# Expert choice stage: fp16 halves with three products, or single fp32 numbers with fp32 products

## The chip, the cores and the metric

The kernel runs on one core of a Trainium2 chip. A core has five engines with queues of their own that meet only at semaphores: TensorE (PE; its weight loads have a row of their own, PEld), VectorE (DVE), ScalarE (ACT), GpSimd (POOL) and SyncE (SP), which here issues nearly all DMAs. Matmul results land in PSUM, everything else is in SBUF. The metric is the device time of one execution in microseconds, as a median over runs.

## The reference

A residual stream `x` of 128 sequences x 64 tokens x 128 features goes through four steps: a gated cross attention (8 heads), a gated expert choice feed-forward, a second cross attention (16 heads) and a routed feed-forward (2 of 8 experts). The change concerns the second step:

```python
b, n, d = x.shape                                   # 128, 64, 128, after a layer norm
gate_logits = jnp.einsum('bnd,ed->ben', x, gate_query)
affinity = _sinkhorn(gate_logits / jnp.exp(log_temp))        # 16 experts
gates, idx = jax.lax.top_k(affinity, CAP)                    # CAP = 32 tokens of each sequence
expert_in = jnp.take_along_axis(x[:, None, :, :], idx[..., None], axis=2)
h = jax.nn.gelu(jnp.einsum('becd,edf->becf', expert_in, w1) + b1[None, :, None, :])   # 128 -> 512
expert_out = jnp.einsum('becf,efd->becd', h, w2) + b2[None, :, None, :]               # 512 -> 128
out = jnp.zeros_like(x).at[jnp.arange(b)[:, None, None], idx].add(gates[..., None] * expert_out)
```

## The kernel before

The program has five stages in a row: attention `a0` (with the expert weights loaded beside it), the Sinkhorn iterations and the top-k (`expert_choice`), `run_experts`, attention `a1`, and the routed layer. `run_experts` is where nearly all of the change lies.

**Numbers in two halves.** An fp32 value is kept as two fp16 numbers, `hi` (the value rounded) and `lo` (the value less `hi`). `matmul3` (L236 to L241) makes a product of three fp16 matmuls, hi·hi, hi·lo and lo·hi. The expert weights are split once, in `a0`: SP loads each expert's `w1` and `w2` into a buffer `rawe`, and POOL writes `hi` by a copy (L809) and `lo` by a subtraction (L812), one such step in each of 64 units; SP waits for POOL (`ew_lo`) before it loads over `rawe`.

**The steps of run_experts.** The 128 sequences make 8 groups of 16. A step is one expert `e` of one group `G`, 128 steps in all, and each covers 16 x 32 = 512 gathered rows. The order on each engine is written out by hand in `body(a)`; a step's work on PE is

- in every second step `take` (L1601): four fp16 matmuls with a one-hot matrix gather the rows of the next tile of tokens into the accumulators `psR` and `psH[:, 3]`;
- the first layer of the next step's expert (L1640): for each `ft` of 4, 128 of the 512 hidden features of 512 rows into the bank `psH[:, ft]`;
- the second layer of this step's expert (L1650): 4 row blocks `r` x 4 `ft` products of 128x128 into the one bank `psE`;
- in every second step the scatter of the last two experts (L1674): one-hot matrices `put` times the gated rows `eo` are added up in `psA`, in pairs for the two halves of 64 partitions.

ACT makes `g32` by the gelu of each `psH` bank (L1722) and rounds two of them at a time to `h` hi (L1727); it also makes the hi halves of the gated rows (L1706) and of the gathered rows (L1710). DVE makes the lo halves: of `h` (L1803, twice a step), of the gated rows (L1821) and of the gathered rows (L1773). DVE further makes `put` (L1816), `sel` (L1761) and the gating (L1830), which copies `psE` out times the gates. PE waits for `h_lo` and for `gated` of the step before ahead of the second layer, for `eo_lo` and `put` ahead of the scatter. `h`, `put` and `eo` have two buffers, `psE` and `eo32` have one.

Ahead of the steps, for the 8 tiles of the first group (L1611 to L1620, `take_early`), PE gathers rows into the four `psH` banks, two for hi and two for lo, ACT copies three of them out and DVE one.

## Time and profile before

| | us |
|---|---|
| median of 3 runs | 1879.14 (1878.74 to 1879.46) |
| the profiled execution | 1880.83 |
| its span, first to last instruction | 1878.1 |
| first matmul of `run_experts`' steps to the last of its scatter | 476.8 to 1256.8 |

| engine | busy over the span | share |
|---|---|---|
| PE | 1796.1 | 96% |
| DVE | 1613.5 | 86% |
| ACT | 1548.2 | 82% |
| POOL | 662.4 | 35% |

The mean granted clock of TensorE is 0.978 of full. PE's busy time counts a matmul from its start to the end of its way through the array, so two that overlap are counted once, and the distance of starts in a stream (called the pitch below) is much shorter than the duration of one: what a stream costs is its count times its pitch. POOL is idle in the whole of `run_experts`.

### The profile page before, as it was taken

To read this page: it belongs to the slowest core of one execution; us is meant where nothing else is said; L and a number is where in the kernel's file an instruction comes from. 1 tells how busy PE (TensorE), PEld (TensorE's weight loads), DVE (VectorE), ACT (ScalarE), POOL (GpSimd) and SP (SyncE) were. 2 spreads that over 40 slices of the span, in tenths; PEclk is the share of its full clock that TensorE was granted. 3 is DMA by queue.
4 is the path that set the end of the run, shared out by engine and by line. 5 is a ranking of instruction groups with operands and counts; after the bars stand their busy time and mean duration, and the time that the engine had idled before them with its cause. 6 is when DMAs were issued, how large, how long until landed. Compare 5 with 4: busy or idle time off the path is not lost. (4 is left out here: it accounts for less than half of the span.)

```text
span 1878.1 us, 72670 instructions
## 1 busy us (share of the span) xinstructions
PE 1796.1 (96%) x28635; PEld 1312.8 (70%) x28635; DVE 1613.5 (86%) x3645; ACT 1548.2 (82%) x2773; POOL 662.4 (35%) x918
## 2 busy tenths in 40 slices
PE   6999998896999999999999999989999999999898
PEld 4777776642577777777776777766777777777587
DVE  5999998598788888889898988778999999988754
ACT  5999997475999999999999999868888888888443
POOL 3788887332000000000000000006666666655565
PEclk9999999897999999999999999999999999999799
DMA  6645444487000000000000002005665555533233
GB/s 174 141 95 101 96 94 88 152 307 270 15 13 15 13 15 13 13 13 12 16 10 18 10 15 50 2 15 128 165 158 154 147 152 152 146 71 69 64 116 120
DMA packets 312953, 160.66 MB, mean 86 GB/s; under 512 B 236558, under 2 KB 295862, under 8 KB 312374
## 3 DMA queue, kind: packets, MB, share of 16 engines
q1 hardware_dynamic: 312278, 157.95, 32.1%
q8 instruction: 129, 2.11, 0.5%
q14 instruction: 66, 0.54, 0.1%
q10 hardware_dynamic: 480, 0.05, 0.0%
HBM read 62.33 MB, written 36.83 MB: 53 GB/s over the span
## 5 line engine op out<-in xcount | busy, mean ns | idle before, releaser
L240 PEld LDWEIGHTS psE<-ew,h 128*128 128x128 f16 x6144 | 353.3, 98 | 33.4 <-DVE h L1803 4.6
L240 PE MATMUL psE<-ew,h 128*128 128x128 f16 x6144 | 364.0, 219 | 2.2 <-DVE h L1803 2.1
L1803 DVE TENSOR_TENSOR h<-g,h 128x1024 f16<-128x1024 f32 x256 | 312.8, 1222 | 49.8 <-ACT h L1727 47.9
L1722 ACT ACTIVATE g<-psH,eb1T 128x512 f32<-128x512 f32 x512 | 325.0, 679 | 10.3 <-PE psH L240 4.3
L815 POOL TENSOR_TENSOR Ph<-E,Ph 128x512 f16<-128x512 f32 x192 | 222.0, 1156 | 233.6 <-ACT Ph L769 233.6
L1876 POOL MEMSET rbias<- 64x384 f32 x1 | 0.4, 411 | 801.8 <-POOLq L133 801.8
L1727 ACT ACTIVATE h<-g 128x1024 f16<-128x1024 f32 x256 | 270.6, 1057 | 8.2
L721 ACT ACTIVATE vB<-psV 128x512 f16<-128x512 f32 x384 | 225.9, 589 | 51.0 <-PE psV L619 48.8
L842 DVE TENSOR_TENSOR vB<-psV,vB 128x512 f16<-128x512 f32 x384 | 248.2, 677 | 1.1 <-ACT vB L721 1.0
L619 PE MATMUL psV<-shared 96*64 96x512 f16 x1536 | 210.9, 381 | 1.4 <-DVE vB L842 1.3
L821 POOL TENSOR_TENSOR E<-E,rden 128x512 f32<-128x512 f32 x192 | 199.7, 1040 | 15.5 <-DVE rden L853 14.8
L240 PE MATMUL psH<-shared,ew 128*128 128x512 f16 x768 | 178.9, 382 | 0.4 <-DVE xg L1773 0.2
L240 PE MATMUL psH<-xg,ew 128*128 128x512 f16 x768 | 177.5, 379 | 0.4
L674 PE MATMUL psY<-vB,PT 128*64 128x128 f16 x4608 | 164.2, 221 | 4.9 <-DMA PT<-Ph 4.3
L861 DVE TENSOR_REDUCE top<-psS 128x8 f32<-128x512 f32 x192 | 131.7, 686 | 37.3 <-PE psS L698 36.7
L674 PEld LDWEIGHTS psY<-vB,PT 128*64 128x64 f16 x4608 | 144.9, 111 | 19.6 <-DMA PT<-Ph 10.6
L759 ACT ACTIVATE E<-E,zero_col 128x512 f32<-128x512 f32 x192 | 137.9, 718 | 18.6 <-DVE E L864 15.0
L864 DVE TENSOR_TENSOR E<-psS,top 128x512 f32<-128x512 f32 x192 | 132.7, 691 | 7.8
L698 PE MATMUL psS<-shared,xTa 128*64 128x256 f32 x1024 | 134.6, 383 | 2.0 <-DVE E L864 1.9
L240 PEld LDWEIGHTS psH<-shared,ew 128*128 128x128 f16 x768 | 71.3, 98 | 92.2 <-issue 17.5
L851 DVE TENSOR_REDUCE den<-E 128x8 f32<-128x512 f32 x192 | 130.0, 677 | 4.4 <-ACT E L759 3.5
L240 PEld LDWEIGHTS psH<-xg,ew 128*128 128x128 f16 x768 | 70.8, 98 | 88.3 <-issue 11.6
(312 smaller groups left out, 3385.6 us busy)
## 6 DMA issues: line engine op xcount, KB each, us to landing
keys_ahead<-shared SPq DMA_DIRECT2D x52, 512.0 KB, 4.9
shared<-keys_ahead SPq DMA_DIRECT2D x52, 512.0 KB, 3.6
rawe<-in_L_ffn_w_dram SPq DMA_DIRECT2D x32, 256.0 KB, 3.1
wb<-rw SPq DMA_DIRECT2D x64, 128.0 KB, 2.0
idx<-places SPq DMA_DIRECT2D x110, 64.0 KB, 2.6
out_dram<-x SPq DMA_DIRECT2D x7, 512.0 KB, 3.2
context_T<-shared SPq DMA_DIRECT2D x64, 48.0 KB, 2.4
PT<-Ph SPq DMA_TRANSPOSE x192, 2.9
```

The source lines that it names most:

```text
L240: last = e.matmul(to, a, b, start=start and n == 0, stop=stop and n == 2, **flags)
L619: last = e.matmul(a.values(b)[half(hp)], cT[:, a.ring, cl, half(b)], Bw[:, bl, a.g, hp].rearrange("p k d -> p (k d)"), start=n == 0, stop= ...
L674: last = e.matmul(psY[half(b), 0:D], PT[:, a4.par, pl, pair, half(b)], vB[:, a4.par, vl, b, pair, :], start=a4.g == n == pair == 0, stop=a ...
L698: last = e.matmul(psS[half(b), h:h + 4, :], xT[:, a.tp, half(b)], u[:, a.slot, h:h + 4, half(b)], start=True, stop=True)
L721: e.activation(vB[:, a.par, 0, b].rearrange("p k d -> p (k d)"), a.values(b), ACT.Copy).then_inc(s["vh" + name], 1)
L759: e.activation(E[:, a1.four], E[:, a1.four], ACT.Exp, bias=zero_col[:], scale=DH ** -0.5)\
L815: e.tensor_tensor(Ph[:, a2.par, 1].rearrange("p k t -> p (k t)"), E[:, a2.four].rearrange("p h l -> p (h l)"), Ph[:, a2.par, 0].rearrange( ...
L821: e.tensor_tensor(E[:, a1.four], E[:, a1.four], rden[:, a1.par, :].unsqueeze(2).broadcast_to([P, 8, N]), ALU.mult)\
L842: e.tensor_tensor(vB[:, a.par, 1, b].rearrange("p k d -> p (k d)"), a.values(b), vB[:, a.par, 0, b].rearrange("p k d -> p (k d)"), ALU.sub ...
L1722: e.activation(g32[:, ft, :], psH[:, ft, :], ACT.Gelu_apprx_tanh, bias=b1T[:, a.expert(1) * FT + ft:a.expert(1) * FT + ft + 1]).then_inc(s ...
L1727: e.activation(h[:, 1 - par, 0, ft - 1:ft + 1, :], g32[:, ft - 1:ft + 1, :], ACT.Copy).then_inc(s["h_hi"], 1)
L1803: e.tensor_tensor(h[:, 1 - par, 1, 2 * q:2 * q + 2, :], g32[:, 2 * q:2 * q + 2, :], h[:, 1 - par, 0, 2 * q:2 * q + 2, :], ALU.subtract)\
```

## The change

In `run_experts` each value is one fp32 number. The expert weights are loaded by SP straight into their place, and the POOL steps that split them are gone, as are SP's waits for them. `matmul3` of both layers gives way to one fp32 matmul of the same shape. The gelu writes `h` in fp32 itself; the rounding of `h` and both subtractions are gone. The gating writes `eo` in fp32 straight into one of two buffers, with no halves after it; `put` is fp32 too. The gathered rows, still gathered by fp16 matmuls of two halves that add up in one accumulator, are copied out as fp32 by DVE alone (by ACT and DVE in turn ahead of the steps, where `take_early` now adds both halves up in one pair of banks).

```diff
-            self.w1 = sb(c, "ew1", [P, 2, NE, DFF], F16)
-            self.w2 = sb(c, "ew2", [P, 2, NE, FT, D], F16)
+            self.w1 = sb(c, "ew1", [P, NE, DFF], F32)
+            self.w2 = sb(c, "ew2", [P, NE, FT, D], F32)
...
-                        if first and a.on:
-                            turn = a.j.mod(4)
...
-                            if turn % 2 == 0:
-                                wait(e, s["ew1" if turn == 0 else "ew2"], n, 16)
-                                e.tensor_copy(hi, rawe[:, turn // 2]).then_inc(s["ew_hi"], 1)
-                            else:
-                                wait(e, s["ew_hi"], n, 2, turn // 2 - 1)
-                                e.tensor_tensor(lo, rawe[:, turn // 2], hi, ALU.subtract).then_inc(s["ew_lo"], 1)
...
-                                last = matmul3(e, psH[:, ft, :],
-                                               [w1[:, hl, a.expert(1), ft * P:ft * P + P] for hl in range(2)],
-                                               [a.rows(hl, 1) for hl in range(2)])
-                                last.then_inc(s["H"], 1)
+                                e.matmul(psH[:, ft, :], w1[:, a.expert(1), ft * P:ft * P + P], a.rows(1),
+                                         start=True, stop=True).then_inc(s["H"], 1)
...
-                            wait(e, s["h_lo"], j, 2)
+                            wait(e, s["gelu"], j, FT)
...
-                                    last = matmul3(e, psE[:, r, :],
-                                                   [h[:, par, hl, ft, r * P:r * P + P] for hl in range(2)],
-                                                   [w2[:, hl, a.expert(0), ft, :] for hl in range(2)],
-                                                   r == ft == 0, ft == FT - 1, skip_group_check=True)
+                                    last = e.matmul(psE[:, r, :], h[:, par, ft, r * P:r * P + P],
+                                                    w2[:, a.expert(0), ft, :], start=r == ft == 0,
+                                                    stop=ft == FT - 1, skip_group_check=True)
...
-                                    for hl in range(2):
-                                        for bp in range(2):
-                                            rows = slice(64 * bp, 64 * bp + 64)
-                                            last = e.matmul(psA[:, bp, r, :], put[rows, buf, r, :], eo[rows, buf, hl, r, :],
+                                    for bp in range(2):
+                                        rows = slice(64 * bp, 64 * bp + 64)
+                                        last = e.matmul(psA[:, bp, r, :], put[rows, buf, r, :], eo[rows, buf, r, :],
...
-                                e.activation(g32[:, ft, :], psH[:, ft, :], ACT.Gelu_apprx_tanh,
+                                e.activation(h[:, 1 - par, ft, :], psH[:, ft, :], ACT.Gelu_apprx_tanh,
...
-                            low_rows(a)
+                            wait(e, s["g"], a.t, 2)
+                            side, bank = (1, psH[:, 3, :]) if a.bp == 0 else (0, psR[:])
+                            e.tensor_copy(rows_of(a, side), bank.rearrange("p (e c) -> p e c", c=CAP))\
+                             .then_inc(s["g_1"], 1)
...
-                            wait(e, s["eo_lo"], j - 1)
+                            wait(e, seeded["A"], j - 2)
...
-                            e.tensor_tensor(eo32[:], psE[:], g4.unsqueeze(2).broadcast_to([P, RT, D]),
+                            e.tensor_tensor(eo[:, par], psE[:], g4.unsqueeze(2).broadcast_to([P, RT, D]),
```

PE's order in two steps in the midst of the first group, first before and then after. `shared` holds the gathered rows of the even groups, `ew_1` the expert weights; the number behind the x is that of matmuls in a row.

```order
L1674 MATMUL psA<-eo,put 128x128 x32
L1606 MATMUL psR<-sel,xne 128x512
L1606 MATMUL psH<-sel,xne 128x512
...
L240 MATMUL psH<-shared,ew_1 128x512 x12
L240 MATMUL psE<-ew_1,h 128x128 x48
```

```order
L1655 MATMUL psA<-eo,put 128x128 x16
L1593 MATMUL psR<-sel,xne 128x512
L1593 MATMUL psH<-sel,xne 128x512
...
L1625 MATMUL psH<-shared,ew_1 128x512 x4
L1633 MATMUL psE<-ew_1,h 128x128 x16
```

Nothing changes its place on PE: a third of the matmuls of both layers stands there, and half of those of the scatter.

DVE's order over one step with a tile to gather, before and then after, with `h` the hidden values, `xg` the gathered rows and `eo` the gated rows.

```order
L1773 TENSOR_TENSOR xg<-psH,xg 128x16x32
L1747 TENSOR_SCALAR xnfe<-x,mean,rstd 128x128
L1816 TENSOR_SCALAR put<-iota,tok_slot 128x128 x4
L1821 TENSOR_TENSOR eo<-eo_1,eo 128x512
L1803 TENSOR_TENSOR h<-g_1,h 128x1024
L1761 TENSOR_SCALAR sel<-idx_1,token_of_p 128x512
L1830 TENSOR_TENSOR eo_1<-psE,gate_slot 128x512
```

```order
L1760 COPY xg<-psH 128x16x32
L1712 TENSOR_SCALAR xnfe<-x,mean,rstd 128x128
L1769 TENSOR_SCALAR put<-iota,tok_slot 128x128 x4
L1726 TENSOR_SCALAR sel<-idx_1,token_of_p 128x512
L1778 TENSOR_TENSOR eo<-psE,gate_slot 128x512
```

The three subtractions of DVE are gone or have become the one copy, and the rest has kept its order.

## Rows read from the trace of the kernel before

**Rows 1.** Stretches: length, busy PE, PEld, DVE, ACT, POOL; then clock, DMA share, GB/s.
```profile
476.80:484.90 8.10, 7.07 (x26) 2.65 (x24) 3.71 (x6) 6.74 (x11) 0.00 (x0) 0.79 0.08 26
484.90:1253.90 769.00, 767.05 (x9955) 554.25 (x9956) 673.87 (x1378) 709.25 (x1052) 0.00 (x0) 1.00 0.05 15
```

**Rows 2.** All waits of PE from 500 to 1200: total us, times, longest.
```profile
PE psE L240 <- DVE h L1803: 0.2, 1, 0.2
```

**Rows 3.** Timeline of PE, two steps: start, us, work [idle].
```profile
700.86 2.75 PE L240 MATMUL psH<-shared,ew 128*128 128x512 f16 x12
703.45 2.84 PE L240 MATMUL psE<-ew,h 128*128 128x128 f16 x48
706.23 1.07 PE L1674 MATMUL psA<-eo,put 64*128 64x128 f16 x32
707.13 0.38 PE L1606 MATMUL psR<-sel,xne 64*128 64x512 f16 x1
...
707.66 2.76 PE L240 MATMUL psH<-shared,ew 128*128 128x512 f16 x12
710.26 2.84 PE L240 MATMUL psE<-ew,h 128*128 128x128 f16 x48
712.94 0.81 PE L240 MATMUL psH<-shared,ew 128*128 128x512 f16 x3
```

**Rows 4.** Groups of PE, whole span: weights, moving operand, count, busy us, mean ns.
```profile
L240 PE MATMUL psE<-ew,h 128*128 128x128 f16 x6144 | 364.0, 219 | 2.2 <-DVE h L1803 2.1
L240 PE MATMUL psH<-shared,ew 128*128 128x512 f16 x768 | 178.9, 382 | 0.4 <-DVE xg L1773 0.2
L698 PE MATMUL psS<-shared,xTa 128*64 128x256 f32 x1024 | 134.6, 383 | 2.0 <-DVE E L864 1.9
```

**Rows 5.** Timeline of PE, three streams of fp32 matmuls in other stages.
```profile
411.61 1.12 PE L1426 MATMUL psZ<-raws,wTs 64*96 64x128 f32 x16
...
1803.30 1.04 PE L2174 MATMUL psHr<-wb,xTr 128*64 128x128 f32 x16
...
1805.54 0.60 PE L2156 MATMUL psTr<-ident,gr 128*128 128x128 f32 x4
```

**Rows 6.** Weight loads of three lines: ns min/median/max, first and last start.
```profile
L240 PEld LDWEIGHTS psE<-ew,h x6144: 95/98/99, 484.9 to 1253.9; 128*128 128x128 f16 x199
...
L2174 PEld LDWEIGHTS psHr<-wb,xTr x512: 132/137/231, 1766.0 to 1869.4; 128*64 128x64 f32 x171
...
L1426 PEld LDWEIGHTS psZ<-raws,wTs x32: 156/160/160, 411.6 to 431.8; 64*96 64x96 f32 x32
```

**Rows 7.** Groups of DVE and ACT: count, busy us, mean ns, idle before.
```profile
L1803 DVE TENSOR_TENSOR h<-g,h 128x1024 f16<-128x1024 f32 x256 | 312.8, 1222 | 49.8 <-ACT h L1727 47.9
L1727 ACT ACTIVATE h<-g 128x1024 f16<-128x1024 f32 x256 | 270.6, 1057 | 8.2
L1722 ACT ACTIVATE g<-psH,eb1T 128x512 f32<-128x512 f32 x512 | 325.0, 679 | 10.3 <-PE psH L240 4.3
L1830 DVE TENSOR_TENSOR eo<-psE,gate_slot 128x512 f32<-128x512 f32 x128 | 88.3, 690 | 41.3 <-PE psE L240 41.2
L1821 DVE TENSOR_TENSOR eo<-eo,eo 128x512 f16<-128x512 f32 x128 | 87.4, 683 | 0.0
```

**Rows 8.** Timeline of the intake and of both ends of the steps, [idle before].
```profile
471.00 1.58 ACT L1690 ACTIVATE shared<-psH 128x512 f16<-128x512 f32 x3 [0.22 <-PE psH L1597]
...
484.91 0.29 PE L240 MATMUL psE<-ew,h 128*128 128x128 f16 x2 [1.04 <-DVE h L1803]
...
1251.32 2.85 PE L240 MATMUL psE<-ew,h 128*128 128x128 f16 x48 [0.92 <-DVE h L1803]
...
1256.43 0.62 PE L1674 MATMUL psA<-eo,put 64*128 64x128 f16 x16 [1.71 <-DVE eo L1821]
```

**Rows 9.** Attention a0: a POOL group, and a PEld group from 40 to 310.
```profile
L812 POOL TENSOR_TENSOR ew<-rawe,ew 128x512 f32 x26 | 30.2, 1160 | 0.0
...
L619 PEld LDWEIGHTS psV<-Bw,shared 96*64 96x64 f16 x696 | 36.1, 110 | 27.5 <-DVE vB L842 8.8
```

More of the change, by code:

```diff
@@ L535, in body @@
                                 n = a.j.div(4)
-                                wait(e, s["ew_lo"], n, 2, -2)
                                 load_w2(e, n)
@@ L1523, in group, with rows, gathered @@
                     return self.G + (self.e + off) // NE
-                def rows(self, hl, off):
-                    return xg[self.group(off) % 2][:, hl, self.expert(off), :]
-            def gathered(parity, hl, batch):
-                return xg[parity][:, hl, :, CAP * batch:CAP * batch + CAP]
+                def rows(self, off):
+                    return xg[self.group(off) % 2][:, self.expert(off), :]
+            def gathered(parity, batch):
+                return xg[parity][:, :, CAP * batch:CAP * batch + CAP]
             def rows_of(at, side):
                 parity = (at.G + 1 + at.k // GT) % 2
-                return [gathered(parity, hl, (at.k % GT) * 2 + side) for hl in range(2)]
+                return gathered(parity, (at.k % GT) * 2 + side)
             def all_steps(eng, body):
@@ L1591, in batch_rows, with take_early @@
                         e.matmul(psR[:], pick[:, par, :], idx16[:], start=True, stop=True).then_inc(s["R"], 1)
-                    def take_early(k, hl):
-                        for side in range(2):
-                            q = slice(64 * side, 64 * side + 64)
-                            last = e.matmul(psH[:, 2 * hl + side, :], first_tiles[q, k, hl, :], sel[q, k % 2, :],
-                                            start=True, stop=True)
-                        last.then_inc(s["g"], 1)
+                    def take_early(k):
+                        for hl in range(2):
+                            for side in range(2):
+                                q = slice(64 * side, 64 * side + 64)
+                                last = e.matmul(psH[:, 2 * (k % 2) + side, :], first_tiles[q, k, hl, :], sel[q, k % 2, :],
+                                                start=hl == 0, stop=hl == 1)
+                        last.then_inc(s["g"], 2)
                     def take(par):
@@ L1668, in body @@
                                 wait(e, s["put"], j - n, RT)
[L1669 removed]
+                                wait(e, s["gated"], j - n)
                                 for r in range(RT):
[L1671 to L1676 removed]
+                                    for bp in range(2):
+                                        rows = slice(64 * bp, 64 * bp + 64)
+                                        last = e.matmul(psA[:, bp, r, :], put[rows, buf, r, :], eo[rows, buf, r, :],
+                                                        start=False, stop=a.e == NE and n == 1,
+                                                        skip_group_check=True)
                                 last.then_inc(s["A"], 1)
@@ L1686, in high, with first_rows @@
                         e.activation(xn[:, k % 2, 0], xnf[:, k % 2], ACT.Copy).then_inc(s["x_hi"], 1)
-                    def first_rows(k, hl, side):
-                        wait(e, s["g"], Step(None, 0, k), 2, hl - 1)
-                        return e.activation(gathered(0, hl, 2 * k + side),
-                                            psH[:, 2 * hl + side, :].rearrange("p (e c) -> p e c", c=CAP), ACT.Copy)
+                    def first_rows(k):
+                        wait(e, s["g"], Step(None, 0, k), 2)
+                        e.activation(gathered(0, 2 * k + 1), psH[:, 2 * (k % 2) + 1, :].rearrange("p (e c) -> p e c", c=CAP),
+                                     ACT.Copy).then_inc(s["g_1"], 2)
                     for k in range(GT):
@@ L1695, in _ @@
                             high(GT)
-                        first_rows(k, 0, 0)
-                        first_rows(k, 0, 1).then_inc(s["g_1"], 1)
-                        first_rows(k, 1, 1).then_inc(s["g_1"], 1)
+                        first_rows(k)
                     def body(a):
                         j, par = a.j, a.par
-                        if a.has(-1):
-                            wait(e, s["gated"], j - 1)
-                            wait(e, seeded["A"], j - 3)
-                            e.activation(eo[:, 1 - par, 0], eo32[:], ACT.Copy).then_inc(s["eo_hi"], 1)
-                        if a.has_tile(0):
-                            wait(e, s["g"], a.t, 2)
-                            side, bank = (1, psH[:, 3, :]) if a.bp == 0 else (0, psR[:])
-                            e.activation(rows_of(a, side)[0], bank.rearrange("p (e c) -> p e c", c=CAP), ACT.Copy)\
-                             .then_inc(s["g_1"], 1)
                         for ft in range(FT):
@@ L1765, in first_rows @@
                         wait(e, s["g"], Step(None, 0, k), 2)
-                        e.tensor_copy(gathered(0, 1, 2 * k), psH[:, 2, :].rearrange("p (e c) -> p e c", c=CAP))\
-                         .then_inc(s["g_0"], 2)
-                    def low_rows(a):
-                        side, bank = (1, psH[:, 3, :]) if a.bp == 0 else (0, psR[:])
-                        high, low = rows_of(a, side)
-                        wait(e, s["g_1"], a.t, 2, a.bp - 1)
-                        e.tensor_tensor(low, bank.rearrange("p (e c) -> p e c", c=CAP), high, ALU.subtract)\
+                        e.tensor_copy(gathered(0, 2 * k), psH[:, 2 * (k % 2), :].rearrange("p (e c) -> p e c", c=CAP))\
                          .then_inc(s["g_0"], 1)
```

70 lines of the change are left out of this document (21 added, 49 removed).

## The prediction

> **What bounds the kernel now.** I read the busy times by stretch first. In the 769 us of the expert steps PE is busy for 767.05 us at full clock, ACT for 709.25 and DVE for 673.87 [rows 1]. Three engines are near full, so busy time alone does not say which sets the pace; the waits do. From 500 to 1200 PE waits once, for 0.2 us [rows 2], while DVE sat idle for 47.9 us until ACT's `h` came [rows 7]. So PE's stream sets the time, and the timeline shows it unbroken: two steps take 712.94 − 700.86 = 12.08 us [rows 3]. ACT and DVE are close behind, but what they give up is worth only what PE waits for them. The question is then what an fp32 product costs PE against three fp16 ones.
>
> **What the fp16 products cost.** From the starts in [rows 3]: the first layer takes 2.59 us for 12 matmuls of 512 columns, a pitch of 216 ns. The second layer takes 2.68 us for 48 matmuls of 128 columns (710.26 to 712.94), 56 ns each. The scatter takes 0.90 us for 16 pairs, 56 ns a pair. The gather with what follows it takes 0.53 us and does not change. Check: 2 × 2.59 + 2 × 2.68 + 0.90 + 0.53 = 11.97; the other 0.1 is one late weight load between second layer and scatter, where 706.23 − 703.45 is 2.78, not 2.68. Another of 0.09 is inside the 0.53. Both stand where the array goes from full height to halves or back.
>
> **What an fp32 product costs.** Two things must be read, since no fp32 matmul of before has the new shapes.
> First, the number of records. The scores of the attention (L698) are four matmuls a unit in the source; for the 128 units of `a1` that is 512, and the trace has 1024 records of them [rows 4]. So an fp32 matmul is two passes.
> Second, the pitch of a pass. An fp32 pass of 256 columns lasts 383 ns, an fp16 one of 512 columns 382 [rows 4]: two cycles a column. The streams agree. 16 fp32 passes of 128 columns, in eight pairs beside each other, take 1.04 us; less 0.27 for the last one's duration that is 0.77 over seven pitches, 110 ns at L2174 [rows 5]; the L1426 stream, whose pairs split the rows as the scatter's do, gives (1.12 − 0.27) / 7 = 121 with the wait for its first load of 160 ns [rows 6] in it. 110 is twice the 56 ns. A whole fp32 matmul costs four cycles a column where three fp16 matmuls cost three.
> I take 109 ns for a pass of 128 columns. A pass of 512 columns is 1024 cycles, 427 ns at 2.4 GHz, and the fp16 pitch of 216 for 512 cycles has 2 to 3 ns on top: 429 ns.
>
> **The sum, for two steps.** First layer: 8 matmuls are 16 passes × 429 = 6.86 us, was 5.18: +1.68. Second layer: 32 matmuls are 64 passes × 109 = 6.98, was 5.36: +1.62. Scatter: 16 matmuls are 32 passes, 16 pairs × 109 = 1.74, was 0.90: +0.84. The two late loads become longer: fp32 loads last 137 and 160 ns for 64 and 96 columns [rows 6], 23 ns for 32 more, so about 185 for 128, an estimate, against 98: +0.09 each, +0.18. Together +4.32, so 16.4 us in place of 12.08. Over 64 pairs of steps: +276 us.
>
> **What is removed beside it.** The 256 roundings on ACT (270.6 us), the 256 subtractions of `h` (312.8) and the 128 of `eo` (87.4) go, with their like for the gathered rows [rows 7]. PE waited for them at three places at the ends only: 1.04 us before the first second layer, 0.92 and 1.71 near the last ones [rows 8]. The last of these is the gating's two halves, one of them a subtraction of 0.68 [rows 7], and I let about 1.3 of it go. Together −3.3 us. Everywhere else this cover is worth nothing, for PE did not wait.
> The new work of DVE is hidden. Before a step it needs the copy of the gathered rows (about 0.68 us, the time of a subtraction of the same size at L1821 [rows 7]), which PE awaits only ahead of `ft` 3, 2.6 us after the gather. The gating now waits for the scatter of two experts before, since `eo` has two buffers. That is new: behind it on DVE stand `split_tile` and the next copy. The wait ends half of a scatter (0.9 us) after the second layer; gating takes 0.69 more [rows 7], and PE next needs it 3.4 us of first layer later. No stall; if it did come, it would be under 1 us in each pair.
> The intake ahead of the steps goes by ACT's three copies, 1.58 + 0.22 us of idle for each of 8 tiles [rows 8]. One copy is left on ACT, but PE and DVE still hand each tile to and fro, with one copy, one comparison and one pick on DVE: I take −0.5 in all, with 0 and −5 as ends.
> In `a0` POOL loses 64 steps, the subtractions of 1160 ns among them [rows 9]. PE's loads wait 8.8 us there for DVE's `vB`, in part since the two share time; I take −2 and keep 0 and −6 as ends. The DMAs are as many and as large, and SP only loses waits.
>
> Sum: +276 − 3.3 − 0.5 − 2 = +270. Against the profiled execution's own 1880.83 (span 1878.1) that is 2151; the median of the runs is 1.7 lower: **2149 us**.
>
> **A rule and the row.** The streams above have weights of 64 or 96 columns; the second layer's have 128. The one fp32 stream with 128 columns, L2156, runs at (0.60 − 0.27) / 3 = 110 ns [rows 5], but those are transposes, so its loads may be of another kind. The Trainium skill (TensorE: Matmul & The Clock Gate, The mechanism) says that a weight load overlaps with a running matmul only when it goes to other rows of the array. By that rule a full-height load could not hide. For fp16 the trace speaks against it: loads of 98 ns run at a pitch of 56 [rows 3, 6]. The same page (Weight-path perf modes) says that fp32 weights don't get the fast load, and (LDWEIGHTS) that a load takes its columns over 1.2 GHz, by which 128 columns would be an estimate of 107 ns, just under the pitch that I use. The rule gives the first rival below.
>
> **The rivals.**
> *The load of 128 fp32 columns isn't hidden.* Then a pass of the second layer and of the scatter takes the load's length, 185 ns by the extrapolation above, not 109. For: load and pass are nearly equal, and no row has both at 128 columns. Against: 160 ns loads run at 110 in L1426, so a good part of their length isn't occupancy. Price: 4096 passes and 1024 pairs × 76 ns = +389, 2540 us. Chance 0.06.
> *An fp32 pass costs less than I read: one cycle a column.* This one ends faster. It is decided at the point where an fp32 product costs what three fp16 ones do, 648 ns for 512 columns and 168 for 128. Were the two cycles due to PSUM or the narrow weights of those stages and a pass of full weights ran at 216 and 56, PE would need 2 × (1.73 + 1.79) + 0.9 + 0.5 = 8.4 us for two steps, still above DVE's and ACT's new load (ACT eight gelus of 0.68, 5.4 us [rows 7]). Price: 64 × (8.5 − 12.08) = −229, 1650 us. Rows with wide and with narrow weights speak against it. Chance 0.02.
> *The three terms come out right, but TensorE's clock falls to the lower level for parts of the steps.* In rows it was low only where PE had been waiting (0.79 in the first 8 us [rows 1]), and PE now waits less. If a tenth of the steps were at half speed: +105, 2255. Chance 0.03.
> *PE isn't held by the products at all, and the time stays.* It needs slack in PE's stream that the rows don't show. 1879 ± 4. Chance 0.01.
>
> **How the numbers follow.** The forecast has 0.88. Its own range: a pitch of 111 instead of 109 adds 10 us, an occasional wait for the gating or the longer `put` 10 more; late loads that stay at 98 ns take 12 off, `a0` another 4, a shorter stay at the low clock 3. That is 2125 to 2172, which leaves out the rivals and a little of the forecast itself. A difference under 0.2% (4 us) can't be told from none here. Faster by more: 0.02. Within: 0.01. Slower: 0.97.
>
> **What would show it.** In the trace of after: PE without waits in the steps, DVE and ACT busy about half the time; records of the first layer 429 ns apart, of the second 109, pairs of the scatter 109; two steps in 16.4 us; a0 within a few us of before. It would be wrong if passes of the second layer stood 150 or more apart, if the granted clock fell, or if PE waited for gated rows.

## The result, and the profile of the kernel after

The kernel after takes **2161.27 us** (median of 4 runs, 2156.89 to 2164.07); the kernel before, run between them, took 1878.94 (4 runs). The ratio is 1.1501, with a 95% interval of 1.1481 to 1.1521. The forecast was 2149 with a range of 2125 to 2172: right in sign and nearly in size, 12 us too low. The profiled execution took 2161.61 us, its span 2159.3, against 1880.83 and 1878.1 before.

The first lines of the page of after, busy time and the span in 40 slices:

```profile
PE 2077.0 (96%) x26075; PEld 1542.3 (71%) x26075; DVE 1252.0 (58%) x3261; ACT 1185.1 (55%) x2261; POOL 609.0 (28%) x854
...
PE   6999998969999999999999999999899999999898
...
DVE  5999985972333332333333333221599999998754
ACT  5999984733333333333333333333488888888643
...
PEclk9999998989999999999999999999999999999899
```

In the long middle part, the expert steps, PE stays at 9 while ACT falls to 3 and DVE to 3 or 2. The same by stretches, to be held against [rows 1] (columns: the stretch and its length, then the busy time of PE, PEld, DVE, ACT and POOL with their instructions, the granted clock, the DMA share, GB/s). The first piece is the first 7 us of the steps:

```profile
472.40:479.40 7.00, 7.00 (x18) 3.15 (x17) 2.19 (x5) 4.89 (x8) 0.00 (x0) 1.00 0.14 40
479.40:1532.30 1052.90, 1052.84 (x7405) 779.08 (x7403) 320.47 (x995) 358.50 (x563) 0.00 (x0) 1.00 0.04 10
```

PE is busy for 1052.84 of 1052.90 us at full clock. DVE's 320.47 and ACT's 358.50 are 30% and 34% of that, where before they had 88% and 92%. The clock is at its upper level from the first step on; before it was 0.79 in the first 8 us [rows 1].

The waits from 490 to 1500 us (who waits, for whom: us in total, times, longest). Before, PE waited there once, for 0.2 us [rows 2]; now no row has PE in it, none of its weight loads (PEld) names another engine, and the three longest waits are for PE:

```profile
ACT h L1692 <- PE psH L1625: 668.1, 435, 6.5
DVE eo L1778 <- PE psA L1655: 359.4, 61, 6.9
DVE eo L1778 <- PE psE L1633: 297.8, 61, 6.5
```

Two steps on PE, the counterpart of [rows 3]: L1625 is the first layer, L1633 the second, L1655 the scatter, L1593 the gather (columns: start us, length us, what, number of records):

```profile
800.09 3.70 PE L1625 MATMUL psH<-shared,ew 128*128 128x512 f32 x8
803.63 3.73 PE L1633 MATMUL psE<-ew,h 128*128 128x128 f32 x32
807.20 3.60 PE L1625 MATMUL psH<-shared,ew 128*128 128x512 f32 x8
810.63 3.73 PE L1633 MATMUL psE<-ew,h 128*128 128x128 f32 x32
814.30 2.06 PE L1655 MATMUL psA<-eo,put 64*128 64x128 f32 x32
816.19 0.38 PE L1593 MATMUL psR<-sel,xne 64*128 64x512 f16 x1
...
816.72 0.70 PE L1625 MATMUL psH<-shared,ew 128*128 128x512 f32 x1
```

From 800.09 to 816.72 are 16.63 us, where it had been 12.08; 16.4 was forecast. A step's first layer is 4 matmuls in the source and has 8 records, its second 16 and has 32: two passes for each fp32 matmul, as read. From the starts, the two first layers take 3.54 and 3.43, the second 3.57 and 3.67, the scatter 1.89, the gather and what follows 0.53, the same as before.

The second layer's and the scatter's own groups (columns: line, engine, operation, shapes, count; busy us, mean ns of one; idle time before it). A load of 128 fp32 columns lasts 192 ns, a bit more than the 185 extrapolated from [rows 6]:

```profile
L1633 PE MATMUL psE<-ew,h 128*128 128x128 f32 x4096 | 478.0, 275 | 0.1
L1633 PEld LDWEIGHTS psE<-ew,h 128*128 128x128 f32 x4096 | 477.4, 192 | 61.0 <-issue 61.0
...
L1655 PE MATMUL psA<-eo,put 64*128 64x128 f32 x2048 | 131.4, 278 | 0.5 <-DVE put L1769 0.5
```

Taken over all starts in the trace, records of L1625 stand 429 ns apart, those of L1633 111.6, the pairs of L1655 111.9. The first is exactly the forecast. The other two are above the 109 taken from two cycles a column.

**Where the 281.2 us of span came from**, by the starts and ends of the stages in both traces:

| stretch | before | after | change | forecast |
|---|---|---|---|---|
| up to the intake (mostly a0) | 461.4 | 459.9 | −1.5 | −2 |
| intake | 15.4 | 12.6 | −2.8 | −0.5 |
| the steps | 780.0 | 1062.5 | +282.5 | +276 − 3.3 |
| all behind them | 621.2 | 624.2 | +3.0 | 0 |

The last line can't be put down to the change, which has no code there: in the other kernels below that stretch took from 618.8 to 623.0 us, so one trace of each kernel doesn't tell 3 us from scatter.

### The profile page after: what moved, and what is told of

It reads as the page before. It is cut to its first block and busy times, and to the rows that moved or that the text cites. A ratio compares the mean times of both kernels' runs of the same rounds, so it can differ in the third digit from the quotient of the medians.

```text
span 2159.3 us, 65740 instructions
## 1 busy us (share of the span) xinstructions
PE 2077.0 (96%) x26075; PEld 1542.3 (71%) x26075; DVE 1252.0 (58%) x3261; ACT 1185.1 (55%) x2261; POOL 609.0 (28%) x854
## 3 DMA queue, kind: packets, MB, share of 16 engines
q8 instruction: 109, 1.79, 0.3%
## 5 line engine op out<-in xcount | busy, mean ns | idle before, releaser
L1692 ACT ACTIVATE h<-psH,eb1T 128x512 f32<-128x512 f32 x512 | 351.9, 687 | 691.3 <-PE psH L1625 691.2
L1633 PEld LDWEIGHTS psE<-ew,h 128*128 128x128 f32 x4096 | 477.4, 192 | 61.0 <-issue 61.0
L1778 DVE TENSOR_TENSOR eo<-psE,gate_slot 128x512 f32<-128x512 f32 x128 | 88.5, 692 | 691.4 <-PE psA L1655 372.5
L1633 PE MATMUL psE<-ew,h 128*128 128x128 f32 x4096 | 478.0, 275 | 0.1
L1625 PE MATMUL psH<-xg,ew 128*128 128x512 f32 x512 | 233.6, 599 | 0.0
L1625 PE MATMUL psH<-shared,ew 128*128 128x512 f32 x512 | 233.4, 599 | 0.0
L1625 PEld LDWEIGHTS psH<-shared,ew 128*128 128x128 f32 x512 | 92.3, 190 | 105.9 <-issue 105.9
L1625 PEld LDWEIGHTS psH<-xg,ew 128*128 128x128 f32 x512 | 92.2, 190 | 103.0 <-issue 102.0
L757 ACT ACTIVATE E<-E,zero_col 128x512 f32<-128x512 f32 x192 | 137.8, 718 | 18.8 <-DVE E L851 15.4
L1655 PE MATMUL psA<-eo,put 64*128 64x128 f32 x2048 | 131.4, 278 | 0.5 <-DVE put L1769 0.5
```

The source lines that it names most:

```text
L757: e.activation(E[:, a1.four], E[:, a1.four], ACT.Exp, bias=zero_col[:], scale=DH ** -0.5)\
L1625: e.matmul(psH[:, ft, :], w1[:, a.expert(1), ft * P:ft * P + P], a.rows(1), start=True, stop=True).then_inc(s["H"], 1)
L1633: last = e.matmul(psE[:, r, :], h[:, par, ft, r * P:r * P + P], w2[:, a.expert(0), ft, :], start=r == ft == 0, stop=ft == FT - 1, skip_gro ...
L1692: e.activation(h[:, 1 - par, ft, :], psH[:, ft, :], ACT.Gelu_apprx_tanh, bias=b1T[:, a.expert(1) * FT + ft:a.expert(1) * FT + ft + 1]).the ...
```

## The experiments

Every kernel was compared with the kernel before on the same chip (1878.66 for the first four, 1879.71 for the next four, 1880.67 for the last). The theory was the forecast's: time is the number of PE's passes times their pitch, and the rest is off the path. Its first weak place was named in the prediction: whether a pass of 128 fp32 columns is spaced by its stream or by its load.

**Each part alone.** Three kernels start from before and take one part of the change each.

*The first layer alone*, with the gathered rows as single fp32 numbers copied by DVE:

```diff
-                                last = matmul3(e, psH[:, ft, :],
-                                               [w1[:, hl, a.expert(1), ft * P:ft * P + P] for hl in range(2)],
-                                               [a.rows(hl, 1) for hl in range(2)])
-                                last.then_inc(s["H"], 1)
+                                e.matmul(psH[:, ft, :], w1[:, a.expert(1), ft * P:ft * P + P], a.rows(1),
+                                         start=True, stop=True).then_inc(s["H"], 1)
```

> The kernel before with the first layer alone in fp32 (expert w1, gathered rows, intake), second layer and scatter in fp16 halves. If the time is PE's stream and the terms add up: the trace of after has 16 passes of 429 ns and one late load of 0.1 us more in two steps, 6.97 us against 5.18, so +1.79 x 64 = +115 us, less some 5 for the intake and the start: 1879 + 110 = 1989. By the prediction's own term it would be +107 - 3: 1983. Rival: the parts don't add up, since each alone leaves ACT and DVE nearly as busy as before and PE then waits for them: over 2000.

*The second layer alone*, where the gelu writes `h` as fp32:

```diff
-                                    last = matmul3(e, psE[:, r, :],
-                                                   [h[:, par, hl, ft, r * P:r * P + P] for hl in range(2)],
-                                                   [w2[:, hl, a.expert(0), ft, :] for hl in range(2)],
-                                                   r == ft == 0, ft == FT - 1, skip_group_check=True)
+                                    last = e.matmul(psE[:, r, :], h[:, par, ft, r * P:r * P + P],
+                                                    w2[:, a.expert(0), ft, :], start=r == ft == 0,
+                                                    stop=ft == FT - 1, skip_group_check=True)
```

> The kernel before with the second layer alone in fp32 (w2, h; no rounding of h, no subtraction). PE's stream: 64 passes of 111.6 ns, 7.14 us against 5.36 in two steps, +1.78 x 64 = +114, less 3 at the ends: 1990. By the prediction's pitch of 109 it would be +104 - 3: 1980. The pitch of the passes says which: 111 to 112 or 109. Rival: the relief of ACT (270 us) and DVE (313 us) gives something back and it comes out under 1975.

*The scatter alone*, with `eo` and `put` in fp32:

```diff
-                                    for hl in range(2):
-                                        for bp in range(2):
-                                            rows = slice(64 * bp, 64 * bp + 64)
-                                            last = e.matmul(psA[:, bp, r, :], put[rows, buf, r, :], eo[rows, buf, hl, r, :],
...
+                                    for bp in range(2):
+                                        rows = slice(64 * bp, 64 * bp + 64)
+                                        last = e.matmul(psA[:, bp, r, :], put[rows, buf, r, :], eo[rows, buf, r, :],
```

> The kernel before with the scatter alone in fp32 (put, eo; no halves of eo). PE's stream: 1.89 us against 0.90 in two steps, +0.98 x 64 = +63, less 2 at the end: 1940. By the prediction's term +0.84 + 0.09: +60 - 2 = 1937. The three single parts together should give the whole change, +282: rival, the whole is more or less than the sum of its parts by over 15 us.

Measured, each a median of four: 1987.93 (ratio 1.0582, 1.0564 to 1.0600), 1987.58 (1.0580, 1.0563 to 1.0598) and 1936.69 (1.0313, 1.0296 to 1.0331), so +109, +109 and +58 us. Together that is +276 of the +282 of the whole. The parts add up, as they must if one engine's stream is the only thing that counts; a part that had been hidden under another's wait would have shown as a gap here. Most of the 6 us between them has a source in the traces. The steps of the three kernels grow by 111.7, 108.2 and 58.7 us, where 64 times what two of their steps grow by would be 117.3, 114.0 and 63.0. So each sheds 4 to 6 us of small waits and low clock, 16 in sum, where the whole can shed its 9 only once. One step of the first and of the second on PE:

```profile
805.11 3.70 PE L1639 MATMUL psH<-xg,ew 128*128 128x512 f32 x8
808.65 2.84 PE L240 MATMUL psE<-ew,h 128*128 128x128 f16 x48
811.33 3.65 PE L1639 MATMUL psH<-xg,ew 128*128 128x512 f32 x8
```

```profile
805.60 2.76 PE L240 MATMUL psH<-xg,ew 128*128 128x512 f16 x12
808.20 3.73 PE L1650 MATMUL psE<-ew,h 128*128 128x128 f32 x32
811.77 2.75 PE L240 MATMUL psH<-xg,ew 128*128 128x512 f16 x12
```

In the first, the fp16 second layer keeps its 2.68 us (808.65 to 811.33); in the second, the fp16 first layer keeps its 2.60 (805.60 to 808.20) and the fp32 second layer has the 3.57 of after. A part's cost hardly depends on the format of its neighbour: two steps grow by 1.83, 1.78 and 0.98 us in the three, 4.60 in sum, and by 4.55 in the whole.

**What the helpers of ACT and DVE were worth.** This kernel starts from before and leaves out the subtractions that make the low half of `h`; PE multiplies the high half in their place, the same number of matmuls.

```diff
-                            wait(e, s["h_lo"], j, 2)
+                            wait(e, s["h_hi"], j, 2)
...
-                                                   [h[:, par, hl, ft, r * P:r * P + P] for hl in range(2)],
+                                                   [h[:, par, 0, ft, r * P:r * P + P] for hl in range(2)],
```

> The kernel before, without DVE's 256 subtractions of h (312.8 us busy); PE makes the same three products with the hi half of h in the place of the lo half. That leaves the lo half of h out of the computation. If DVE's work was covered, as the prediction says, only waits at the ends go: 1876, -1 to -4 us. Rival: DVE and PE share the pace and it comes out 10 us or more faster.

Measured: 1878.61, ratio 0.9993 (0.9981 to 1.0006), so no difference that can be told. From 500 to 1200 us (columns as in the stretches above):

```profile
500.00:1200.00 700.00, 699.74 (x9063) 505.69 (x9060) 357.87 (x1032) 652.69 (x973) 0.00 (x0) 1.00 0.06 16
```

DVE works 51% of the time instead of 88%, and PE's 699.74 us stay. In its profiled execution the steps took 776.7 us against 780.0, 3.3 less. It took 312.8 us of DVE's work away [rows 7] and brought about 1% of it back.

That 3.3 is also the forecast's figure for what is removed beside the products is luck. Of the three waits that made it up, only the 0.92 us before the last second layer is gone here; the one of 1.71 still stands, and one of 1.12 ahead of the first gather of the steps has come for the one of 1.04. Up to the first scatter the kernel gains 0.2 us and after the last but one 1.0. The other 2.1 lie in the midst of the steps, at the changes from one group to the next. At six of these, two steps of before took up to 12.59 us in place of 12.08, in sum 2.8 us more (work that all kernels have there left out); here it is 0.7, in after nothing. The waits of PE's weight loads show it in before, in rows that the prediction hadn't read (500 to 1200 us):

```profile
PEld psH L240 <- ACT g L1722: 2.3, 4, 0.6
PEld psE L240 <- DVE h L1803: 2.0, 4, 0.7
```

Without the subtractions the second is gone and the first is 1.7. It begins with a DMA: at 604 us DVE's `sel` waits 1.62 us for `idx` to land, and the subtraction of `h` behind it is late for PE. So the helpers were not wholly covered, but what they cost was some 3 us of 780.

**What spaces the passes of 128 columns.** If their stream does, passes of 64 columns go twice as fast; if the load of 128 weight columns does, they don't. From after, each matmul of the second layer is cut into two of 64 columns with the same weights:

```diff
-                                    last = e.matmul(psE[:, r, :], h[:, par, ft, r * P:r * P + P],
-                                                    w2[:, a.expert(0), ft, :], start=r == ft == 0,
-                                                    stop=ft == FT - 1, skip_group_check=True)
+                                    for q in (slice(0, 64), slice(64, P)):
+                                        last = e.matmul(psE[:, r, q], h[:, par, ft, r * P:r * P + P],
+                                                        w2[:, a.expert(0), ft, q], start=r == ft == q.start == 0,
+                                                        stop=ft == FT - 1, skip_group_check=True)
```

> The kernel after, with each product of the second layer made as two of 64 moving columns, so that each fp32 pass streams 64 columns (53 ns) behind the same load of 128 fp32 columns; the result is the same. Theory A, the load of 128 fp32 columns is what spaces the passes at 111.6 ns, the stream of 107 just hides under it: the pitch stays near 110, there are 8192 passes, +450 us: about 2610. Theory B, the stream spaces them and loads hide: pitch about 56, time unchanged at 2161. In between, the pitch is the load's own.

Measured in one run: 2610.93 us. On PE and from the line's own view (columns: engine, operation, count; ns min/median/max of one; first and last start; shapes):

```profile
806.95 7.25 PE L1634 MATMUL psE<-ew,h 128*128 128x64 f32 x64
814.13 2.06 PE L1656 MATMUL psA<-eo,put 64*128 64x128 f32 x32
```

```profile
L1634 PEld LDWEIGHTS psE<-ew,h x8192: 186/192/192, 476.0 to 1983.1; 128*128 128x128 f32 x200
L1634 PE MATMUL psE<-ew,h x8192: 219/275/294, 476.4 to 1983.2; 128*128 128x64 f32 x200
```

64 passes take 7.18 us, 112 ns each, though each streams half as many columns. Every pass brings its own load of 128 weight columns, also the second one with the same weights, and these loads come one each 111.6 ns. That settles it: at 128 columns of fp32 the load sets the pitch, at 111.6 ns, not the stream. The first interval of each second layer shows what the stream alone would do, since no load has come within 400 ns ahead of the one for its second pass: 55 to 56 ns here and 109 to 110 in after, in 127 of 128 steps each. From then on passes and loads come 111 to 112 apart in both. A load's record lasts 192 ns and still the next follows after 112, so the length of a record isn't the time for which it holds up the next.

**Narrower loads.** Then loads of 64 columns should bring the pitch back to the stream's two cycles a column. The second layer's rows are split into halves of 64 that stand side by side in the array:

```diff
+                                    for q in (slice(0, 64), slice(64, P)):
+                                        last = e.matmul(psE[q, r, :], h[:, par, ft, r * P + q.start:r * P + q.stop],
+                                                        w2[:, a.expert(0), ft, :], start=r == ft == 0,
+                                                        stop=ft == FT - 1, skip_group_check=True)
```

> The kernel after, with each product of the second layer made as two with 64 weight columns, side by side in the array's column halves, streaming the same 128 columns at once; the result is the same. The load of a pass is then 64 columns (137 ns long, not 192). Theory A, the load spaced the passes: pairs stand 109 to 110 apart as at the routed layer, 4096 x 2 ns less: 2153. Theory B, the 2 ns over 109 have another cause: unchanged, 2161.

Measured: 2180.76 (1.1603, 1.1583 to 1.1622), so 20 us slower than after, not faster. The loads did shorten (192 to 137 ns) and the pairs do stand closer, 109.4 ns on average over the trace against 111.6, but for the first interval of each step, 153. As a pair has two passes and two loads, 111.6 isn't a fixed least time of a pass either. But the step got longer:

```profile
804.15 3.70 PE L1625 MATMUL psH<-shared,ew 128*128 128x512 f32 x8
807.79 3.71 PE L1634 MATMUL psE<-ew,h 128*64 128x128 f32 x64
811.43 3.70 PE L1625 MATMUL psH<-shared,ew 128*128 128x512 f32 x8
815.06 2.19 PE L1634 MATMUL psE<-ew,h 128*64 128x128 f32 x36
```

Both first layers now take 3.64 us (804.15 to 807.79), where after has 3.54 and 3.43, and the second layers 3.64 too, where after has 3.57. The array changes its shape between full and split four times in two steps, in after twice, and at each change the first load can't run ahead. That is 0.10 + 0.21 us of first layers and 2 × 0.07 of second ones, less the 0.1 of late load ahead of the scatter, which now finds the array split already: 0.35 us in two steps, 22 us in all, where 20 were measured. The closer pitch came, the gain that was expected from it didn't: I had the price of the late loads in the prediction and left it out of this one.

**One pass instead of two.** float32r is another format of 32 bits for TensorE's operands; how exact its products are was not measured here. From after, the second layer in it, with `w2` put into it by a copy on POOL during a0 and `h` by the gelu that writes it:

```diff
-            self.w2 = sb(c, "ew2", [P, NE, FT, D], F32)
+            self.w2 = sb(c, "ew2", [P, NE, FT, D], F32R)
...
-            h = sb(c, "h", [P, 2, FT, ROWS], F32)
+            h = sb(c, "h", [P, 2, FT, ROWS], F32R)
```

> The kernel after with the second layer's two operands as float32r (POOL rounds w2 as it lands and copies w1, the gelu writes h rounded), all else as after; products are rounded to that format, so less exact than fp32. Theory A: a float32r matmul is one pass of one cycle a column, and the load of 128 four-byte columns (about 110 ns) is then what spaces the matmuls: 32 x 0.112 = 3.6 us in two steps against 7.14, -228: 1933. Theory B: it is one pass and the loads hide at 56 ns too: -342: 1819. Theory C: it runs in two passes of two cycles like fp32: 2161, no change.

Measured: 1927.39 (1.0258, 1.0241 to 1.0275), 234 us less than after. The timeline has 16 records for the 16 matmuls of a step:

```profile
809.03 3.70 PE L1636 MATMUL psH<-xg,ew 128*128 128x512 f32 x8
812.17 2.30 PE L1644 MATMUL psE<-ew,h 128*128 128x128 f32 x16
```

But for the first, whose record begins early, they stand 111.7 ns apart, the pitch of an fp32 pass. So a matmul of this size costs two loads' pitches in fp32, one in float32r and three times 56 in fp16 halves: 223, 112 and 168 ns. The saving of 234 us is 2048 pitches of 111.6 (229) and a little of late loads.

**A version that beats both.** By these prices the first layer is best left in fp16 halves (648 ns a matmul against 858), the second layer and the scatter are cheapest in float32r. From before:

```diff
-            self.w2 = sb(c, "ew2", [P, 2, NE, FT, D], F16)
+            self.w2 = sb(c, "ew2", [P, NE, FT, D], F32R)
...
-            h = sb(c, "h", [P, 2, 2, FT, ROWS], F16)
-            put = sb(c, "put", [P, 2, RT, P], F16)
+            warm = sb(c, "warme", [P, 1], F32)
+            h = sb(c, "h", [P, 2, FT, ROWS], F32R)
+            put = sb(c, "put", [P, 2, RT, P], F32R)
```

> The kernel before with the first layer as it was (fp16 halves, three products), second layer and scatter with float32r operands, in single passes (less exact than fp32 in both): in two steps 5.18 + 32 x 0.112 + 8 x 0.112 + 0.1 + 0.53 + 0.2 = 10.5 us against 12.08, so -101 and -3 at the ends: 1775, faster than both. Rival: ACT or DVE, still with the halves of the gathered rows, sets the pace above 11 us: over 1805.

Measured: **1757.94 us**, ratio 0.9349 (0.9333 to 0.9365), 6.5% faster than the kernel before. Two steps take 814.15 − 803.89 = 10.26 us:

```profile
803.89 2.76 PE L241 MATMUL psH<-shared,ew 128*128 128x512 f16 x12
806.30 2.09 PE L1653 MATMUL psE<-ew,h 128*128 128x128 f32 x16
808.23 2.76 PE L241 MATMUL psH<-shared,ew 128*128 128x512 f16 x12
...
812.66 1.11 PE L1675 MATMUL psA<-eo,put 64*128 64x128 f32 x16
...
814.15 2.76 PE L241 MATMUL psH<-shared,ew 128*128 128x512 f16 x12
```

PE still waits for nothing between 500 and 1100 us; ACT is busy for 368.37 of the 600, DVE for 300.47. It came out 17 us better than expected. The plain sum by the prices measured above is 2 × 2.59 + 32 × 0.112 + 8 × 0.112 + 0.53 + 0.1 = 10.29 us, and that is what the steps take; what the expectation allowed on top of it wasn't needed.

**The first layer in one pass.** What is a pass of 512 float32r columns? This kernel is for its time only: the first layer multiplies `w1` with `w2`'s numbers in place of the gathered rows, since the rows' memory is shared with other stages that don't write it as float32r. All its work on the other engines is done.

```diff
-                                last = matmul3(e, psH[:, ft, :],
-                                               [w1[:, hl, a.expert(1), ft * P:ft * P + P] for hl in range(2)],
-                                               [a.rows(hl, 1) for hl in range(2)])
-                                last.then_inc(s["H"], 1)
+                                e.matmul(psH[:, ft, :], w1[:, a.expert(1), ft * P:ft * P + P],
+                                         w2[:, a.expert(1)].rearrange("p k d -> p (k d)"),
+                                         start=True, stop=True).then_inc(s["H"], 1)
```

> A timing kernel: all three products of the experts with float32r operands, but the first layer streams the expert's w2 (512 columns) in the place of the gathered rows, which leaves the gathered rows out of the result. It tells what a float32r pass of 512 columns costs, where a load can't be the limit. Theory A, two cycles a column as in one fp32 pass: 429 ns a matmul, 3.43 us for 8 in two steps, with 3.5 for the second layer, 1.05 for the scatter, 0.53 and 0.2: 8.7 us, 1879 - 64 x 3.38 - 6 = 1657. Theory B, one cycle a column: 216 ns, 1.73 us, 7.0 in two steps, 1550 if ACT keeps up with its 5.4 us of gelus.

Measured: 1613.35 (0.8619, 0.8555 to 0.8684), three runs within 1611.8 to 1614.4 and one of 1636.3. The time lies between the two expectations, so the trace has to say which holds. One step:

```profile
803.76 1.14 PE L1636 MATMUL psH<-ew 128*128 128x512 f32 x4
804.80 1.98 PE L1645 MATMUL psE<-ew,h 128*128 128x128 f32 x16
806.71 1.11 PE L1667 MATMUL psA<-eo,put 64*128 64x128 f32 x16
```

Four records for four matmuls, with most starts 227 to 235 ns apart: one pass. One cycle a column would be 213 ns at 2.4 GHz, two would be 427, so it is one, with some 18 ns on top that no run here explains; an fp32 matmul takes 858. Two steps take 7.42 us (800.77 to 808.19). What is missing to the lower expectation is that PE is no longer alone: it starts to wait, and the granted clock falls in several stretches (the waits from 500 to 980 us, then stretches):

```profile
PEld psE L1645 <- ACT h L1704: 11.3, 6, 2.0
PE psE L1645 <- DVE eo L1790: 8.8, 6, 1.6
```

```profile
500.00:600.00 100.00, 98.26 (x752) 81.02 (x750) 63.41 (x196) 63.18 (x114) 0.00 (x0) 0.94 0.06 19
600.00:700.00 100.00, 96.77 (x716) 79.52 (x716) 62.55 (x193) 58.00 (x104) 0.00 (x0) 0.88 0.06 18
...
900.00:980.00 80.00, 80.00 (x670) 69.36 (x669) 46.88 (x159) 55.46 (x94) 0.00 (x0) 1.00 0.12 32
```

The last stretch, where PE is busy without a gap, is at the upper level (2.4 GHz) throughout; the two shown above it, in which PE was idle for 1.7 and 3.2 us, have 0.94 and 0.88 on average, so parts of them at the lower level. The order in the trace is waits first. Between 492 and 889 us PE sits idle seven times for 1.4 to 1.6 us, each time at the upper level, and 0.2 to 2.8 us after each the clock falls to the lower one (1.2 GHz). All seven stand behind a wait of DVE for `idx`, one in each group, of 2.6 to 2.8 us. One of them:

```profile
558.71 0.35 DVE L1738 TENSOR_SCALAR sel<-idx,token_of_p 128x512 f16<-128x512 f16 x1 [2.65 <-DMA idx<-places]
...
559.81 2.40 PE L1645 MATMUL psE<-ew,h 128*128 128x128 f32 x14 [1.46 <-DVE eo L1790]
```

DVE waits for `idx`, its gating `eo` comes late, PE waits for that, and from 560.70 to 567.53 us the clock is at the lower level. In all it is so for 74 of the 517 us of the steps, which costs up to half of that, 37 us by estimate; the idle time is 12.8 us, and two steps at 7.42 instead of 7.0 make 27. These more than cover the 63 us that are missing to 1550; an exact split was not made. With the real gathered rows this kernel wasn't tried.

## Why the prediction was right, and what was mis-sized

**What bounds the kernel.** Right in the main. PE's stream has no wait in the steps of after but one of 0.5 us at their end, the three parts add up to +276 of +282, and 312.8 us less of DVE's work moved the median by nothing that can be told. But "everywhere else this cover is worth nothing" missed the 2.8 us at the changes of group.

**Two passes, two cycles a column.** Right in number and kind: 8 and 32 records a step, and 429 ns for a pass of 512. The first layer's term, +1.68 us in two steps, was measured as +1.79, and the 0.11 is a late load (below).

**109 ns for a pass of 128 columns.** Mis-sized, by a cause I had passed over. I took the pitch from the stream, twice 56 less a little, and treated the load as hidden or not hidden. It is neither: loads run ahead of the running pass, but one after another only each 111.6 ns, which is 2 to 3 ns above what the stream would need. Over 64 second-layer passes that is 0.16 us in two steps and over 16 scatter pairs 0.05, so 13 us in all. The rows that I used, L2156 and L2174 [rows 5], could not show it. Over the whole trace of before, their passes or pairs stand 109 to 110 ns apart, which is the stream's pitch; the loads at L2174 have 64 columns (137 ns), and those of the transposes at L2156 have 128 but last 140 ns, not 192, so they are of another kind, as the prediction allowed. The range did hold a pitch of 111.

The rule that I weighed, that a load overlaps only with a matmul in other rows of the array (the Trainium skill, TensorE: Matmul & The Clock Gate, The mechanism), is contradicted at full height in fp32 too: loads of 192 ns come at a pitch of 111.6. What the same section of the Trainium skill has beside it, that a load also goes ahead when it targets a background weight buffer, the trace does not contradict. The same page of the Trainium skill (LDWEIGHTS) lets a load take its columns over 1.2 GHz, an estimate of 107 ns for 128. In kind, a load with a time of its own, the experiment with halves agrees; in size the measured 111.6 is 5 ns above it.

**The first rival** said that the load would set the pitch and put its price at the load's record, 185 ns. The first half came true and the price didn't. For this reason a rival's price should go by a pitch, and never by the length of a record.

**The late loads.** Right: I had the two late loads of two steps grow by 0.09 each, and they do. It doesn't show where the prediction read them, for the 0.10 ahead of the scatter and the gather's 0.53 are unchanged. It is in the interval behind the first pass. After a change of the array's shape the first pass's record begins with its own load and lasts 697 ns instead of 592 (the 0.70 of the last line of the two steps above), and the next pass of the first layer comes after 533 ns instead of 429: +0.10, where in fp16 it was 227 instead of 216, +0.01. The second pair of the scatter comes 0.10 late in the same way. Together 0.21 against 0.18.

**What is removed beside it.** Less the products, the steps gave 282.5 − 64 × 4.55 = −8.7 us, where −3.3 was forecast. By the starts of the scatters, some 3.3 of it lie ahead of the first one, 3.2 between and 1.9 at the end.

- At the end 2.2 was forecast (0.92 and 1.3): nearly right.
- At the start the wait of 1.04 went, as forecast. The rest is the clock: before, TensorE was at the lower level for the first part of the steps, 3.4 us in all, which costs 1.7 by estimate; in after for none. The prediction had that as an end of its range, 3 us, not in its sum.
- In between, the 2.8 us at the changes of group went, which the prediction put at nothing because it read the waits of PE's matmuls alone and not those of its weight loads.

Why the clock is up when the steps of after begin stays open. The intake's busy time doesn't decide it: PE is busy there for 8.97 of 12.50 us at a mean granted clock of 0.86, before for 12.77 of 15.40 at 0.60, so for the smaller share in after, but the lower clock itself makes the same matmuls longer. All five kernels with the old intake began their steps in part at the lower level, and of the six with the new one two did so too (float32r in the second layer, float32r everywhere).

The intake itself became shorter. Here is one tile of it in after:

```profile
467.18 0.61 PE L1584 MATMUL psH<-sel,xg 64*128 64x512 f16 x4
467.32 0.74 DVE L1726 TENSOR_SCALAR sel<-psR,token_of_p 128x512 f16<-128x512 f32 x1
467.89 0.60 ACT L1671 ACTIVATE shared<-psH 128x512 f32<-128x512 f32 x1 [0.79 <-PE psH L1584]
...
468.11 0.68 DVE L1731 COPY shared<-psH 128x512 f32<-128x512 f32 x1
...
468.57 0.61 PE L1584 MATMUL psH<-sel,xg 64*128 64x512 f16 x4
```

A tile takes 1.39 us instead of the 1.80 of ACT's three copies [rows 8], and the intake 2.8 us less in all; 0.5 was forecast, within ends of 0 and 5.

**Hidden work.** The copies of the gathered rows and the gating cost PE nothing, as forecast: no wait of PE in the steps names them. DVE and ACT are busy for a third of the time, not the half that the prediction named among its signs; its own sum had it already, with eight gelus of 5.4 us in 16.4.

**The sum.** Against the forecast's +270: pitch +13, late loads +2, waits and clock in the steps −5, the intake −2, the stretches ahead of and behind all this +0.5 and +3. That is +11, which gives the 281.2 us of span measured. So products that came 15 too dear, and 3.5 outside of the steps, met 7 that were saved beside them and not foreseen; that errors of both signs met is luck. The terms named for the range add up to 2130 and 2169, its stated ends are 5 and 3 us further out; the measured time lies within both.

## What to carry to other kernels

Where TensorE's stream sets the time, count passes times pitch for each format and matmul size, and take the pitch as the larger of the stream and of the weight load: here three fp16 products of 512 columns cost 648 ns, one fp32 product 858, and at 128 columns 168, 223, and 112 for one float32r. Time that an edit frees on the other engines is worth only what TensorE waited for them, which the list of waits says, if the rows of its weight loads are read beside those of its matmuls. Before splitting a matmul to gain a few ns of pitch, count how often the array then changes its shape: here 128 further changes cost 20 us net of what the split gave, some 0.15 us each, and so more than the split was worth.

## What the runs showed of the hardware that I had not expected

- Loads of 128 fp32 weight columns for matmuls follow each other each 111.6 ns, whether 128 or 64 columns are streamed behind them and though the record of one lasts 192 ns. In the kernel with halves the same weights are loaded again for the second half. For the transposes of L2156 such a load lasts 140 ns and the pitch is 109.
- float32r takes one pass: 231 ns for 512 columns, and 112 for 128, where the load is the limit. fp32 takes two passes of two cycles a column each, 429 ns at 512.
- After a change between full and split array the first load doesn't run ahead, and in fp32 it costs 0.19 to 0.20 us, half of it ahead of the first pass's record and half within it (533 instead of 429 ns to the next record of the first layer); in fp16 it was 0.10.
- In the all-float32r kernel seven waits of PE of 1.4 to 1.6 us, in a stream that was otherwise busy, were each followed by a fall of the clock to its lower level for 3.4 to 20.5 us; the mean granted clock of the stretches of 100 us that hold them was 0.88 to 0.96. In after, where PE doesn't wait between 490 and 1500 us, it was 1.00.
